# VectorE's order in the body of a chunk loop, and another start for its first chunk

## The reference

```python
x = conv_attention(x)                    # q, k, v by 3x3 convs, attention over the images, norm, relu,
                                         # conv 3x3 (Wc), x + result
t = tokens(x)                            # per image: 256 tokens of 128 features
# L1_attn on layernorm(t), S = 8 search heads of 16, R = 2 retrieval heads of 16
search_attn = softmax(einsum('bsid,bsjd->bsij', sq * scale, sk))
retrieved   = einsum('bsij,brjd->bsird', search_attn, rv)
retrieval_attn = softmax(einsum('bsid,bsird->bsir', rq * scale, retrieved @ wk_ret))
t = t + einsum('bsir,bsird->bsid', retrieval_attn, retrieved) @ w_out
# L1_ffn on layernorm(t): 8 experts, the best 2 of them per token
top_logits, top_idx = top_k(z @ Wg, 2);  w = softmax(top_logits)
t = t + sum over the two experts e of w_e * (silu(z @ W1[e]) @ W2[e])
```

## Time and profile before

| | us |
|---|---|
| median of 3 runs | 685.08 (684.0 to 688.95) |
| the profiled execution | 685.38 |
| its span, first to last instruction | 683.6 |
| TensorE busy | 566.0 (83% of the span) |
| VectorE busy | 475.9 (70%) |
| ScalarE busy | 333.1 (49%) |
| GpSimd busy | 262.6 (38%) |

### The profile page before, as it was taken

One profiled execution on the slowest core, in us unless ns is written; L12 is line 12 of the kernel. 1 busy time (PEld: TensorE's weight loads), 2 busy tenths in 40 slices (PEclk: granted clock), 3 DMA queues, 4 the chain that ended last, 5 costly groups with the idle time before them and its releaser, 6 DMA issues. The chain is left out here.

```text
span 683.6 us, 10705 instructions
## 1 busy us (share of the span) xinstructions
PE 566.0 (83%) x3180; PEld 439.7 (64%) x3180; DVE 475.9 (70%) x1227; ACT 333.1 (49%) x718; POOL 262.6 (38%) x328
## 2 busy tenths in 40 slices
PE   5999999849788988979898887876169999999910
PEld 4888888636565767666666665654058888888810
DVE  6886774855557777777878778785537767767715
ACT  3322302233356465554636355544148888888800
POOL 3245443458000100141413314247603666666660
PEclk9999999959879999999999999998569999999965
DMA  7994145649531405041230505001278777776109
GB/s 262 365 347 145 57 170 185 203 164 372 153 116 39 155 1 155 1 151 36 96 92 31 157 3 184 9 25 48 76 251 293 234 243 230 246 235 221 51 6 363
DMA packets 55224, 105.46 MB, mean 154 GB/s; under 512 B 8744, under 2 KB 21689, under 8 KB 55040
## 3 DMA queue, kind: packets, MB, share of 16 engines
q1 hardware_dynamic: 50176, 96.24, 42.6%
q0 software_dynamic: 4992, 8.54, 3.6%
HBM read 58.15 MB, written 48.42 MB: 156 GB/s over the span
## 5 line engine op out<-in xcount | busy, mean ns | idle before, releaser
L1949 POOL DMA_INDIRECT y_slots<-virt,pad_l x92 | 95.7, 1041 | 72.5 <-DVE virt L2001 49.5
L1280 DVE TENSOR_REDUCE s_max<-bank 128x2 f32<-128x512 f32 x128 | 87.4, 689 | 40.3 <-PE bank L1596 39.8
L1059 ACT ACTIVATE s_expd<-bank 128x512 f32<-128x512 f32 x128 | 76.9, 602 | 53.5 <-PE bank L1617 52.3
L973 POOL DMA_INDIRECT x_slots<-rows,slot_of x64 | 63.1, 986 | 55.9 <-DVE rows L1408 38.3
L937 POOL TENSOR_TENSOR ln_rstd<-ln_var,power 128x4 f32<-128x4 f32 x17 | 17.4, 1026 | 173.4 <-DVE ln_var L1256 173.4
L1989 DVE TENSOR_TENSOR k_stack<-virt,k_stack 128x512 fp32r<-128x512 f32 x92 | 63.4, 689 | 24.9 <-ACT k_stack L1968 24.2
L1632 PE MATMUL bank<-s_expd,rvx 128*64 128x256 f32 x512 | 70.5, 397 | 1.5 <-ACT s_expd L1059 1.0
L61 PE MATMUL bank<-pad_h,u_h 128*128 128x512 f32 x144 | 59.9, 416 | 8.4 <-DVE pad_l L399 8.4
L1617 PE MATMUL bank<-q_stack,k_stack 100*128 100x256 f32 x256 | 61.8, 325 | 5.0 <-DVE q_stack L1298 5.0
L1968 ACT ACTIVATE k_stack<-virt 128x512 fp32r<-128x512 f32 x92 | 58.2, 633 | 10.1 <-PE bank L63 7.2
L1963 ACT ACTIVATE virt<-bank 128x512 f32<-128x512 f32 x92 | 55.0, 597 | 14.3 <-PE bank L63 13.9
(11 more groups left out here) (260 smaller groups left out, 1321.8 us busy)
## 6 DMA issues: line engine op xcount, KB each, us to landing
x_slots<-blank SPq DMA_DIRECT2D x8, 2112.0 KB, 17.3
pad_h<-w_split SPq DMA_DIRECT2D x23, 512.0 KB, 4.4
q_stack<-w_split SPq DMA_DIRECT2D x23, 512.0 KB, 5.7
qk_rows<-qk SPq DMA_DIRECT2D x16, 512.0 KB, 3.0
k_stack<-qk_rows SPq DMA_DIRECT2D x96, 64.0 KB, 2.4
q_stack<-qk_rows SPq DMA_DIRECT2D x48, 128.0 KB, 2.6
pad_l<-x_slots SPq DMA_DIRECT2D x23, 264.0 KB, 5.2
e_raw<-in_w SPq DMA_DIRECT2D x16, 256.0 KB, 3.0
```

The lines of the kernel that those rows point to most:

```text
L973: pool.indirect_dma_start(out=x_slots[:, :], out_offset=bass.IndirectOffsetOnAxis(ap=slot_of[:, ring, k, j:j + 1], axis=0), in_=rows[:, ri ...
L1059: nc.scalar.activation(expd[:, s % 4].rearrange("p a i -> p (a i)"), ps_st[s % 2][:, :], ACT.Exp).then_inc(exp_done, 1)
L1280: nc.vector.tensor_reduce(s_max[:, :, s], ps_s[s % 2][:, :].rearrange("p (a j) -> p a j", a=2), AX.X, ALU.max).then_inc(max_done, 1)
L1949: pool.indirect_dma_start(out=y_slots[:, :], out_offset=bass.IndirectOffsetOnAxis(ap=ids, axis=0), in_=y_rows[:, t % 2, j, :], in_offset=N ...
```

## The change

- In the first half of each body but the last, VectorE does parts 1 and 2 of `retrieve(g - 1, 1)` both at s = 2, and the three parts of `route(g - 2)` at s = 4, 5 and 6, behind what else these steps hold, instead of 2, 3 and 4.
- For chunk 0, SyncE issues only bounce k and the two fills of k. ScalarE issues bounce q between its two token copies, and the two fills of q behind `split_zt(1)`, which now comes ahead of `image_pair(6)`.
- The first eight scores go to four banks (`ps_s + ps_st`) instead of two. All nine taps of chunk 2 and its `add_conv` come ahead of them.
- `low(12)` to `low(15)` move from the start into steps 2 to 5 of body 0's first half.

The diff, cut to its core:

```diff
+    first_banks = ps_s + ps_st
...
+    def bounce(queue, g, first, signal):
+        queue.dma_start(qk_rows[bass.ds(g, 1), first:first + 2].rearrange("g n c t -> c (g n) t"),
+                        f32(qk[:, first:first + 2, :])).then_inc(signal, 16)
...
     @block.sync
     def _(sp):
+        def first_stack():
+            sp.wait_ge(k_ready, 1)
+            bounce(sp, 0, 0, k_bounced)
+            sp.wait_ge(k_bounced, 16)
+            fill_k(sp, 0, 0, 0)
+            fill_k(sp, 0, 0, 1)
...
-        stack(0, 0)
+        first_stack()
         stack(1, 1)
...
+        def bounce_first_q():
+            act.wait_ge(q_ready, 1)
+            bounce(act, 0, 2, q_bounced)
+
+        def stack_first_q():
+            act.wait_ge(q_bounced, 16)
+            act.wait_ge(stack_init, 2 * S + 1)
+            fill_q(act, 0, 0, 0)
+            fill_q(act, 0, 0, 1)
...
         keep_tok(0, 0, 0)
+        bounce_first_q()
         keep_tok(0, 1, 0)
+        split_zt(1)
+        stack_first_q()
         image_pair(6)
-        split_zt(1)
         image_pair(7)
...
-        def row_max(g, b, s):
+        def row_max(g, b, s, banks=ps_s):
...
+                if stage == FIRST and s in (2, 3, 4, 5):
+                    low(10 + s)
                 if stage != FIRST:
-                    if s in (1, 2, 3):
+                    if s in (1, 2):
                         retrieve(g - 1, 1, s - 1)
+                    if s == 2:
+                        retrieve(g - 1, 1, 2)
                     if s == 5:
                         add_attention(g - 1)
...
-                if g >= 2 and s in (2, 3, 4):
-                    route(g - 2, ring, s - 2)
+                if g >= 2 and s in (4, 5, 6):
+                    route(g - 2, ring, s - 4)
...
         normalise(1, z_tok, 1)
-        low(12)
-        low(13)
         low_zt(1)
-        low(14)
-        low(15)
+        add_conv(2, ps_pv[0])
         for s in range(S):
-            row_max(0, 0, s)
-            if s == 3:
-                add_conv(2, ps_pv[0])
+            row_max(0, 0, s, first_banks)
...
-            need(pe, max_done, 2 * S * g + S * b + s - 1)
+            need(pe, max_done, 2 * S * g + S * b + s + 1 - len(banks))
...
-        conv_taps(2, range(4, 8), ps_pv[0])
+        conv_taps(2, range(4, 9), ps_pv[0])
         head_k(1)
         for s in range(S):
-            scores(0, 0, s, 0)
-            if s == 0:
-                conv_taps(2, range(8, 9), ps_pv[0])
+            scores(0, 0, s, 0, first_banks)
```

More of the change, by code:

```diff
@@ L877, in max_bank, with fill_k @@
         return ps_x if stage in (FIRST, MIDDLE) else ps_conv
+    first_banks = ps_s + ps_st
     def chunk(tensor, g):
         return tensor[:, bass.ds(g * CH, CH)]
+    def bounce(queue, g, first, signal):
+        queue.dma_start(qk_rows[bass.ds(g, 1), first:first + 2].rearrange("g n c t -> c (g n) t"),
+                        f32(qk[:, first:first + 2, :])).then_inc(signal, 16)
+    def fill_k(queue, g, ring, b):
+        at = slice(b * PIX, (b + 1) * PIX)
+        for slot, n in enumerate((0, 0, 1)):
+            src = qk_rows[bass.ds(g, 1), n, :, at].rearrange("g (p a r) t -> a r (g p) t", p=NP, a=2)
+            for a in range(2):
+                row = 32 * slot + D * a
+                queue.dma_start(f32(k_stack[row:row + D, ring, a:S:2, at]), src[a]).then_inc(stacked[b], 16)
@@ L882, in _, with fill_q @@
+    def fill_q(queue, g, ring, b):
+        at = slice(b * PIX, (b + 1) * PIX)
+        for slot, n in enumerate((2, 3, 2)):
+            src = qk_rows[bass.ds(g, 1), n, :, at].rearrange("g (p r) t -> r (g p) t", p=NP)
+            queue.dma_start(f32(q_stack[32 * slot:32 * slot + 32, ring, :, at]), src
+                            ).then_inc(stacked[b], 16)
     @block.sync
     def _(sp):
-        def stack(g, ring):
[L888 to L906, removed]
@@ L908, in stack @@
+        def first_stack():
[4 more added lines that the diff above has]
+            fill_k(sp, 0, 0, 1)
+        def stack(g, ring):
             sp.wait_ge(k_ready, g + 1)
-            bounce(0, k_bounced)
+            bounce(sp, g, 0, k_bounced)
             sp.wait_ge(q_ready, g + 1)
-            bounce(2, q_bounced)
+            bounce(sp, g, 2, q_bounced)
             sp.wait_ge(k_bounced, 16 * (g + 1))
-            fill_k(0)
+            fill_k(sp, g, ring, 0)
@@ L914, in stack @@
             sp.wait_ge(q_bounced, 16 * (g + 1))
-            fill_q(0)
-            fill_k(1)
-            fill_q(1)
+            fill_q(sp, g, ring, 0)
+            fill_k(sp, g, ring, 1)
+            fill_q(sp, g, ring, 1)
         for e in range(BLANKED_EARLY, NE + 1):
@@ L1276, in low_q @@
             nc.vector.tensor_tensor(q_l, ps_x[:, :], f32(q_h), ALU.subtract).then_inc(q_ready, 1)
-        def row_max(g, b, s):
+        def row_max(g, b, s, banks=ps_s):
             dve.wait_ge(s_done, 2 * S * g + S * b + s + 1)
-            nc.vector.tensor_reduce(s_max[:, :, s], ps_s[s % 2][:, :].rearrange("p (a j) -> p a j", a=2), AX.X,
+            nc.vector.tensor_reduce(s_max[:, :, s], banks[s % len(banks)][:, :].rearrange("p (a j) -> p a j", a=2), AX.X,
                                     ALU.max).then_inc(max_done, 1)
@@ L1587, in head_tokens, with scores @@
                 last.then_inc(tok_done, 1)
-        def scores(g, b, s, ring):
+        def scores(g, b, s, ring, banks=ps_s):
             if s == 0:
                 pe.wait_ge(stacked[b], STACK * (g + 1))
-            need(pe, max_done, 2 * S * g + S * b + s - 1)
+            need(pe, max_done, 2 * S * g + S * b + s + 1 - len(banks))
             at = b * PIX
             for i in range(2):
-                last = pe.matmul(ps_s[s % 2][:, i * PIX:(i + 1) * PIX],
+                last = pe.matmul(banks[s % len(banks)][:, i * PIX:(i + 1) * PIX],
                                  q_stack[0:96, ring, s // 2, at + i * P:at + (i + 1) * P],
```

## The result

| | before | after |
|---|---|---|
| median of 15 runs each, us | 686.27 (683.32 to 691.4) | 681.56 (678.34 to 684.86) |
| the profiled execution, us | 685.38 | 679.69 |
| its span, us | 683.6 | 677.9 |
| mean granted clock of TensorE in it | 0.927 | 0.927 |

The account below looks back on a forecast made before the run. The prediction took TensorE, the busiest engine, as held up by waits for VectorE and the first stacks. Start 3.0, body 1 0.6 and bodies 2 to 5 5.7 made 9.3 us off 685.38: 676 us, range 671.5 to 681.

Parts of the forecast that it names:

- The bodies: VectorE's new order in first halves: 5.7 us from bodies 2 to 5, 0.6 from body 1, 0 from body 6; 6.3 us.
- The rival by which VectorE becomes the bound of the first halves of bodies 2 to 5: First halves: VectorE sets the pace, the bodies keep 2 us or less and 680.5 us comes out; chance 0.12.
- the one by which the reorder does nothing: First halves: the gate of ScalarE, for which part 1 of retrieve waits, is what is late; 682 us, chance 0.03.
- The four banks: Ahead of body 0: eight row maxima take 4.88 us instead of 7.40, a gain of 2.5 us.
- Step (b): Ahead of body 0: q transfers go to ScalarE's queue, first scores at 180.9, a gain of 0.5 us.
- could take twice as long to go out: Ahead of body 0: upper bound for the first q fills when fills on two queues overlap, 1.4 us more.
- the first stacks do not come sooner: Ahead of body 0: ScalarE's queue is later than SyncE's, 1.4 us lost, 677.5 us (679 without the banks' gain); chance 0.12.
- The clock rival: Start of body 0: TensorE's wait shrinks to some 0.6 us, its clock may stay up, 674.5 us; chance 0.2.
- rival on the slower side: Starts of bodies: the clock falls to 1.2 GHz more often, 1.7 us each, from six nothing left of 9.3; chance 0.03.

## Why the forecast's size was off

**The bodies: right.** The wait at `o_tok` was to fall to 0.11 us and fell to 0.22 to 0.35; the stretch behind it was to grow by 0.30 and grew by 0.23. That `m_split` comes 0.15 us ahead of the transposes that need it, so that a part of the gain is lost there, holds too. Without a fall, bodies 2 to 5 went from 37.9 to 38.0 us to 36.6 to 36.8: 1.2 to 1.4 each, where 1.42 was forecast. Body 1 gained 0.5 (0.6). Body 6 gained nothing (0); its first half was 0.1 us longer, and its stall is at `m_split` with 2.64 us (2.6). The rival by which VectorE becomes the bound of the first halves of bodies 2 to 5 fell, and so did the one by which the reorder does nothing.

**The four banks: right.** Eight maxima in 4.87 us (4.88). From the first scores to body 0 it was 10.54 us before and 7.96 after: 2.6, forecast 2.5.

**Step (b), the transfers of q: wrong, first cause.** The forecast had the first q fill issued 4.41 us behind the mark (at 177.1) and the first scores 3.79 us behind that. The issue came sooner, at +3.71 (174.63): the bounce went out at +0.86 where the estimate of 174.0 is +1.31, and it took 2.85 us as forecast. What failed is the stretch to the scores, taken over unchanged from one queue: it was 5.65 us instead of 3.79. With both queues issuing, the q fills landed in 4.7 us instead of 2.8 and the k fills in 3.8 instead of 2.4, since the second halves go out while the first still run. So 0.70 us were gained at the issue and 1.86 lost behind it. The text had this as an upper bound ("could take twice as long to go out", 1.4 us) and then did not carry it into the sum.

In the four kernels with these queues and no other change at the start the first scores came 9.36, 9.39, 9.61 and 10.01 us behind the mark; in the kernel before and in the two with its start, 8.72, 8.74 and 8.59. With the second halves held back it was 8.23, and body 0 began the whole 3.1 us sooner. That this is the forecast's 8.2 to the tenth is luck: the issue was 0.6 us sooner than forecast (+3.78) and the stretch behind it 0.7 longer (4.45 us). So the rival "the first stacks do not come sooner" is what happened, by contention and not by a late queue, and it cost 1.1 us of the forecast. The rule of the Trainium skill that the forecast cited here (page "DMA: Bandwidth & Descriptors", section "Issuing engines are not separate DMA queues") speaks of this: transfers issued from several engines run on the same 16 DMA engines. By that rule the trace agrees: the busy share of the DMA engines in the 6 us ahead of the first scores rose from 0.63 to 0.95, while what they moved went from 178 to 192 GB/s only, and each fill took longer.

**The clock: wrong, second cause.** The sum took for granted that TensorE's clock falls as it did before. Two things did not hold. The clock rival expected that the fall ahead of body 0 might not come, since the wait there would shrink to 0.6 us; the wait stayed at 2.21 us and a second of 2.23 us followed behind the scores, and body 0 gave back 0.7 us. With matmuls in these waits it was 1.00 over 182 to 188, but 0.72 over the 6 us behind that. And the starts of bodies 3 to 5 all ran at 1.2 GHz, where one had. Each fall cost 1.0 to 1.5 us, which is what the forecast had as its rival on the slower side, there at 1.7 us each, at a chance of 0.03, and only as a case so bad that nothing is left. It belonged into the sum as one or two falls more. That waits lower the clock is also what the Trainium skill's page "TensorE: Matmul & The Clock Gate" says in the section that the forecast cited; here it was applied to the start only, while the 1.6 us wait at the end of each body was taken as given because the change doesn't touch it.

**What the 3.4 us are.** They can't be added up from one pair of profiles, which differ by 3.9 us from the common mark where the runs give 5.9. What the runs and profiles say of each part:

- The transfers: 1.1 us at the first scores. The kernel with held-back halves has 1.6 us less in the median, with intervals that overlap, and 0.5 us less at the end of body 0.
- The order: in the two kernels with the matmuls added, bodies 1 to 6 gained 7.1 us, 5.6 without the old order's one fall. That is 0.7 less than the 6.3 of the forecast.
- The clock: the mean granted clock over all runs is 0.925 before (the 32 runs of the experiments) and 0.922 after (15), which is some 3 us more at the lower level. Over the 32 runs of the kernel before the time rises by 0.35 us for each of them (correlation 0.94), so 1 us. Body 0's 0.7 us is a part of that.

That is 2.3 to 2.8 us. What is left, 0.6 to 1.1 us, the interval of the ratio (1.7 us to each side) doesn't tell from nothing.

**What stays open** is by what way the new order brings more time at the lower clock. At the starts of bodies 3 to 6, behind a wait of 1.6 us, the profiles of the two kernels with the old order and unfilled waits have 3 falls in 8; those of the four with the new order and no relief at the ends of the bodies have 13 in 16. The mean clock over all their runs says the same on more counts: 0.925 and 0.926 in the first two (32 and 12 runs), 0.920 to 0.923 in the other four (39 runs), which is 4 us more at the lower level. But filling the waits brought nearly the same 5 to 6 us to both orders, which speaks against a large effect. No run shows the way from the one to the other.

## What to carry to other kernels

Work out a moved transfer to its landing, not to its issue: a second queue saves issue time, but transfers that nobody needs yet, issued behind the urgent ones, slow those; hold them back. Where TensorE waits for one or two microseconds in every round of a loop, look at the granted clock behind each wait and put the possible falls into the range, and then shorten the wait rather than fill it: moving five small instructions brought 6 to 7 us, as much as the whole change. Compare two profiles from the last common, unchanged instruction, not from the start of the span.

## What the runs showed of the hardware that was not expected

- TensorE's clock falls behind a wait of 1.6 us in some rounds and not in others that look the same: in the kernel with the new order alone, bodies 3, 4 and 6 but not 5. A wait of 0.85 us was followed by no fall in any of four rounds, nor was the wait of 0.95 us ahead of bodies 1 and 2 in the profiles that have it. The length of the wait alone does not decide it: in the middle of body 6 of the kernel before, the clock fell behind a wait of 0.93 us (0.79 over the next 8 us).
- 116 matmuls that nobody reads made the changed kernel 6.2 us faster, and 110 made the kernel before 5.6 us faster, by the medians.
- At body 0's start they held the clock in the one (1.00 over 182 to 194 in the kernel before with them) and only put the fall off in the other (1.00 over 182 to 188, 0.72 over 188 to 194).
- ScalarE issues a transfer in 0.46 us of its own time (2.77 for six), as SyncE does (5.52 for twelve), and its work stands still meanwhile: its next instruction comes at 177.45, behind 2.63 us of idle time.

```profile
177.45 1.09 ACT L1011 ACTIVATE virt<-virt,norm_b,norm_a 128x256 f32<-128x256 f32 x2 [2.63 <-issue]
```
